# The last token block of every state is multiplied by C on GpSimd for 32 states of a chunk instead of 28

## The reference, cut to what matters

```python
def step(h, inp):
    xt, dtt, Bt, Ct = inp
    dA = jnp.exp(dtt[:, :, None] * A[None])
    h = h * dA + (dtt * xt)[:, :, None] * Bt[:, None, :]
    y = jnp.einsum('bds,bs->bd', h, Ct)
    return (h, y)
...
y = y + xc * D_param[None, None, :]
y = y * _silu(z)
return y @ W_out
```

## Time and profile before

| | us |
|---|---|
| median of three runs | 5358.08 |
| lowest, highest | 5353.32, 5359.78 |
| the profiled execution | 5360.15 |
| its span, first to last instruction | 5358.4 |
| VectorE busy | 4683.7 (87%) |
| GpSimd busy | 3950.6 (74%) |
| ScalarE busy | 2778.3 (52%) |
| TensorE matmul busy | 4918.4 (92%) |

### The profile page before, as it was taken

One profiled execution on the slowest core, in us unless ns is written; L12 is line 12 of the kernel. 1 busy time (PEld: TensorE's weight loads), 2 busy tenths in 40 slices (PEclk: granted clock), 3 DMA queues, 4 the chain that ended last, 5 costly groups with the idle time before them and its releaser, 6 DMA issues.

```text
span 5358.4 us, 80481 instructions
## 1 busy us (share of the span) xinstructions
PE 4918.4 (92%) x22548; PEld 3285.4 (61%) x22548; DVE 4683.7 (87%) x5835; ACT 2778.3 (52%) x4598; POOL 3950.6 (74%) x2047
## 2 busy tenths in 40 slices
PE   5899999999999789999999999989989999998967
PEld 2688888888888555555555555555555555555544
DVE  9676676666666599999999999999999999999997
ACT  3111111111111476677667677677767766767754
POOL 5233333333333499999999999999999999999996
PEclk9999999999999899999999999999999999999979
DMA  4111111111111323333333232323223233333222
GB/s 117 40 40 43 43 39 43 43 39 43 43 39 40 111 91 98 100 96 95 95 98 102 91 99 91 117 86 100 91 95 112 85 102 98 101 93 98 80 90 66
DMA packets 302204, 427.90 MB, mean 80 GB/s; under 512 B 38593, under 2 KB 132801, under 8 KB 297714
## 3 DMA queue, kind: packets, MB, share of 16 engines
q1 hardware_dynamic: 301810, 423.44, 25.7%
HBM read 350.94 MB, written 72.40 MB: 79 GB/s over the span
## 4 chain that ended last, share of the span: by engine, by line
PE 18%; DVE 17%; issue 13%; ACT 8%; POOL 7%; DMA 1%; DVEq 1%; SPq 1%; POOLq 0%; ACTq 0%
DVE hs L1412 11%; DVE acc L1426 6%; PE mm L1534 4%; POOL v L1181 4%; PE ht L1546 4%; ACT decay L1371 3%; PE mm L1477 3%; PE mm L1486 3%; PE mm L1494 2%; PE mm L1518 1%; POOL hw L1191 1%; PE yw L1556 1%; DMA b_rep<-ssm_d 1%; DVEq L1023 1%; ACT L1267 1%
## 5 line engine op out<-in xcount | busy, mean ns | idle before, releaser
L1181 POOL TENSOR_TENSOR v<-u,b_rep 128x1024 f32<-128x1024 f32 x1024 | 2402.8, 2367 | 130.2 <-DVE hs L1412 71.8
L1371 ACT ACTIVATE decay<-dt,a_neg 128x512 f32<-128x512 f32 x2048 | 1391.9, 688 | 775.3 <-DVE hs L1412 750.6
L1546 PEld LDWEIGHTS ht<-ident,hs 128*128 128x128 f32 x6400 | 784.3, 144 | 1073.7 <-issue 678.4
L1412 DVE TENSOR_TENSOR_SCAN hs<-decay,carry,v 128x512 f32<-128x512 f32 x1024 | 1284.3, 1271 | 32.4 <-ACT decay L1371 14.7
L1412 DVE TENSOR_TENSOR_SCAN hs<-decay,v 128x512 f32<-128x512 f32 x1024 | 1222.0, 1210 | 35.5 <-ACT decay L1371 14.7
L1546 PE MATMUL ht<-ident,hs 128*128 128x128 f32 x6400 | 1010.4, 282 | 217.9 <-DVE acc L1426 99.8
L1426 DVE SCALAR_TENSOR_TENSOR acc<-ht,c_now,acc 128x512 f32<-128x512 f32 x1600 | 1162.9, 727 | 17.8 <-PE ht L1546 16.7
L686 ACT ACTIVATE sg<-gate 128x512 f32<-128x512 f32 (+1 forms) x192 | 108.0, 563 | 1335.4 <-PE up L732 1335.4
L1191 POOL TENSOR_TENSOR hw<-hs,c_rep 128x512 f32<-128x512 f32 x448 | 573.0, 1279 | 10.4 <-DVE hs L1412 10.4
L1534 PE MATMUL mm<-w_out,yt 128*128 128x512 f32 x1024 | 508.3, 602 | 8.3 <-ACT xb L1252 5.2
L1494 PE MATMUL mm<-w_in,x_z 128*128 128x512 f32 x1024 | 502.0, 598 | 0.0
(11 more groups left out here) (155 smaller groups left out, 7974.6 us busy)
## 6 DMA issues: line engine op xcount, KB each, us to landing
b_rep<-ssm_d SPq DMA_DIRECT2D x512, 256.0 KB, 3.5
w_out<-in_L_attn_W_out SPq DMA_DIRECT2D x32, 1024.0 KB, 7.3
rtb<-res_d SPq DMA_DIRECT2D x128, 256.0 KB, 4.1
tap_diag<-tap_d SPq DMA_DIRECT2D x120, 256.0 KB, 3.6
c_rep<-ssm_d SPq DMA_DIRECT2D x448, 64.0 KB, 3.4
xt<-in_L_attn_x SPq DMA_DIRECT2D x64, 256.0 KB, 2.8
xnt_d<-xntb SPq DMA_DIRECT2D x64, 256.0 KB, 2.7
rt<-in_L_attn_x SPq DMA_DIRECT2D x64, 256.0 KB, 2.6
```

Source lines behind the costliest of these rows:

```text
L1181: nc.gpsimd.tensor_tensor(v[k % 2][:, j:j + 2, :], u[g][:, j:j + 2, :], b_rep[k % 3][:, :].unsqueeze(1).broadcast_to([P, 2, CL]), ALU.mult ...
L1371: nc.scalar.activation(decay[n % 3][:, :], dt[g][:, j, :], ACT.Exp, scale=a_neg[:, GD * g + j, s:s + 1]).then_inc(decay_ready, 1)
L1412: nc.vector.tensor_tensor_scan(h[k % 3][:, j, :], decay[n % 3][:, :], v[k % 2][:, j, :], carry[:, s, GD * g + j:GD * g + j + 1] if c.secon ...
L1546: last = nc.tensor.transpose(ht[add_no[k, t] % 2][:, j, :], h[k % 3][:, j, t * P:(t + 1) * P], ident[:, :])
```

## The change

GpSimd weighs block 3 of all 32 states of a chunk. VectorE adds blocks 0 to 2 alone, 96 `add_state` a chunk instead of 100, and `add_weighed` waits for the start value of `acc` instead of the last sum of block 3. The states 5, 9, 27 and 29 are weighed in the slots 7, 11, 29 and 31; their adds stood in the same slots of VectorE, behind scan 0.

```diff
-    WEIGHED = (0, 1, 2, 3, 4, 6, 7, 8, 10, 11, 12, 13, 14, 15, 16, 17, 18, 19, 20, 21, 22, 23, 24, 25, 26, 28, 30, 31)
+    WEIGHED = tuple(range(SLOTS))
...
-                wait(pool, summed, sums(o, NS * g + NS - 1, j + 1))
+                wait(pool, summed, sums(o, NS * g + NS - 1, min(j + 1, LT - 1)))
...
-            if s == 0 or (t == LT and all((NS * g + i, t) not in add_no for i in range(s))):
+            if s == 0:
...
             wait(dve, w_turned, c.at(NW, weighed_until[g + 1]))
-            wait(dve, summed, sums(c, NS * g + NS - 1, LT))
+            wait(dve, acc_set, c.at(8, 4 * g + 4))
```

## The result

The changed kernel takes 5419.57 us (median of four runs, 5416.59 to 5421.33) beside 5358.93 of the kernel before: a ratio of 1.0114, 95% interval 1.0101 to 1.0127. That is 61 us slower. The prediction was 5396 us with a range up to 5416, so it had the direction and missed the size. The profiled execution's span is 5419.5 us.

A forecast was written before the change was run, and what follows sets the result against it. The prediction took the path as VectorE's from slot 0 to about 22 and GpSimd's from there to the boundary. Its terms, 29.8 - 22.1 + 15 + 15 = +38 us, gave 5396 us, range 5368 to 5416.

The forecast's parts named there:

- What bounds the kernel: Mamba phase: the path is VectorE's from slot 0 to about 22, then GpSimd's to the boundary, 10 times in 15.
- The price of a weighing: On GpSimd, by distances of starts: a weighing costs 1.23 us.
- The price of an add: On VectorE, by distances of starts: an add is worth 0.65 us.
- part 2: Slots 7 and 11: two removed adds save VectorE 1.3 us a chunk, -22.1 us with the last chunk.
- Part 1: Slots 29 and 31 to the boundary: GpSimd's path lengthens, 24.6 us at ten boundaries, 5.2 at five others, sum +29.8.
- part 3: Slot 12: GpSimd's margin shrinks, VectorE stands 2.1 us for `v` in even chunks; +15 us, bounds 0 and 20.
- the prediction's sign: VectorE's slots 7 and 11 would take 6.43 us in even chunks if the prediction was right.
- Part 4: TensorE's queue in slot 12: slot 13's add 1.3 us late in even chunks, 0.6 in odd; +15 us, bounds 0, 25.
- Part 5: TensorE's transposes, C loads, `add_weighed`: no cost; late weighings of states 27 and 29 hidden by VectorE's boundary wait.
- the first: Rival: only the boundary and the adds count, GpSimd keeps enough in hand in slot 12; +7.7 us, 5366, chance 0.13.
- GpSimd on the path throughout: Rival: GpSimd leads throughout, all its 64 weighings on the path; 79 us, 5437, chance 0.07.
- a lock: Rival: GpSimd and VectorE exclude each other at SBUF; if adds did, GpSimd's `v` would show it; no time given.

The follow-up runs named there:

- Experiment 1: The changed kernel with only states 5 and 9 newly weighed, 27 and 29 left to VectorE, and five C buffers: 5381.9 us, ratio 1.0046.
- Experiment 2: The changed kernel with only states 27 and 29 newly weighed on GpSimd, 5 and 9 added by VectorE: 5397.1 us, ratio 1.0076.
- experiment 4: The changed kernel with sp and du of slot 11 moved to slot 13: 5390.3 us, ratio 1.0062.
- Experiment 3: The changed kernel with the 1 MB x_z load issued in slot 1 of the next chunk instead of slot 31: 5404.3 us, ratio 1.0087.
- experiment 5: The changed kernel with TensorE's turn of a weighed state two steps later in its queue (LATE 4 instead of 2): 5396.9 us, ratio 1.0072.

## Why the prediction was right and where it was wrong

- **What bounds the kernel** held: the path is VectorE's up to slot 22 and GpSimd's from there to scan 0. Experiments 1, 2 and 4 show it by place.
- **The price of a weighing** held: 2.39 to 2.47 us for two at each of the ten ordinary boundaries (2.46 forecast). **The price of an add** did not: see part 2.
- **Part 1** is the step that failed by most. "At the five others 1.4 us of it is slack on average" was right as a reading, and the slack was used. The step took for granted that GpSimd's own idle time at the turn stays 0.56 us. It became 3.5 on average (31.8 less the first wait of 14.4 us, over five), because GpSimd got to the branch after x_z was issued and no longer before: 19.1 us instead of 5.2. The prediction's own numbers hold this shift: x_z follows VectorE's pace and was issued 2.6 us behind the start of `u`; GpSimd gets 2.46 us later and VectorE 1.3 earlier, which makes it 1.2 ahead, and 1.1 is measured. Experiment 3 takes 14 us away and leaves 4.8.
- **Part 2 and part 3** held to 0.2 us in sum, and in part by luck. In chunk 6 the first scan of slot 12 comes 0.78 us later than before, for 2.1 - 1.3 = 0.8 forecast, but both terms were too large. In odd chunks the two removed adds give 1.14 us, not 1.3. In even chunks the one of slot 7 gives 0.24 us, not 0.65: the slot takes 6.85 us where the prediction's sign was 6.43, since the next scan now waits for ScalarE's `decay` (the row below), a path that the prediction had not counted. ScalarE starts that `decay` at 3218.10, behind two activation table loads of 1.28 us each. Against that the stand for `v` in slot 12 was 1.8 us and not 2.1, and slots 0 to 7 of chunks 2 and 14 were 0.6 and 1.2 us shorter, for which the runs show no reason.

```profile
3218.89 1.23 DVE L1412 TENSOR_TENSOR_SCAN hs<-decay,v 128x512 f32<-128x512 f32 x1 [0.31 <-ACT decay L1371]
```

- **Part 4** had the mechanism (experiments 4 and 5) and too small a size: 27.2 instead of 15.2. The term counted TensorE's work behind the wait at the durations it had before. In five chunks the clock fell to 0.50 behind the 2.2 us wait, which doubled them and made a second add late: 2.9 to 3.4 us a chunk instead of 1.3, together 9.7 of the 12 us that are missing. Most of the rest is the odd chunks' half clock near slot 18, which the kernel before has too, in fewer chunks. Where the clock kept up, the term is near what was forecast: 1.2 and 1.7 us in even chunks, 0.6 in odd ones. Part 4's upper bound of 25 for all chunks was under the result too.
- **Part 5** held as far as the stretches show: none is left over for the C loads, the transposes or the late states 27 and 29; no run varies them by themselves.
- **The rivals.** Scans do wait for `v` in slot 12, against the first; experiment 4 rules out GpSimd on the path throughout; and GpSimd's `v` takes 2367 ns in the mean before and after the change, so nothing of a lock shows.
- The two missing terms have one sign and one cause: both times the prediction kept a neighbour's time (a fetch, a matmul) as it was, while moving the moment at which it happens.

## What to carry to other kernels

When a shared step moves later, price also what it moves past: the instruction and DMA queues at a loop branch can be shorter or longer by some microseconds according to what was issued just before. A wait that TensorE has in front of a chain is to be priced with the chain at the lower clock as a bound. And where two engines hand the path to each other, the place of a piece of work decides its cost: the same 64 weighings cost 61 us, and 17 with one load and one pair of products moved. With the boundary reordered as well the kernel is level with the one before, but the same order without the change is 12 to 16 us faster, so the cost is smaller and not gone.

## What the hardware showed that was not expected

GpSimd's way over the loop branch, from its last instruction's start to the next turn's first, took 2.8 to 3.1 us at 35 turns with the 1 MB load issued 1.5 to 3.0 us behind that start, and 5.3 to 6.8 us at 25 turns with the load 0.7 to 1.1 us ahead of it. The instruction queue's packet that came 1.0 us after that start at the short turns was late at the long ones. Of two waits of TensorE of equal length in the same place (2.23 and 2.26 us), one was followed by a granted clock of 0.50 and one by 1.00; what decides between them the rows here do not show.
